# Turning probabilities and xn by VectorE blocks and DRAM instead of on PE, in an attention and FFN block

## What is computed

```python
q, k, v = ln(x) @ Wq, ln(x) @ Wk, ln(x) @ Wv
scores = where(above_diagonal, -max, q @ k.T)          # per batch, 1024 x 1024
x = x + ln(softmax(scores / 16) @ v @ Wo)
x = x + ln(ln(x) @ W[idx] + b[idx])
```

## Time and profile before

| | |
|---|---|
| three runs | 425.57, 426.01, 428.9 us (median 426.01) |
| span of the profiled execution (its own run time is not listed apart) | 424.3 us |
| PE, PEld | 414.0, 393.2 us busy |
| VectorE (DVE), ScalarE (ACT), GpSimd (POOL) | 339.8, 299.1, 118.3 us busy |
| DMA | 18.46 MB in 18951 packets, mean 44 GB/s |

### The profile page before, as it was taken

How to read it: one execution, slowest core, us unless ns; L and a number is a source line. 1 busy time by engine, 2 the same in 40 slices (tenths; PEclk the granted TensorE clock), 3 DMA queues, 4 the chain that set the end, 5 groups by cost and what they waited for, 6 DMA issues and landing times.

```text
span 424.3 us, 9812 instructions
## 1 busy us (share of the span) xinstructions
PE 414.0 (98%) x3045; PEld 393.2 (93%) x3045; DVE 339.8 (80%) x1010; ACT 299.1 (71%) x854; POOL 118.3 (28%) x237
## 2 busy tenths in 40 slices
PE   7999999999999999999999999999999999999993
PEld 7789999999999999999999999999999999999993
DVE  4578778987898878887788878898788887876776
...
DMA packets 18951, 18.46 MB, mean 44 GB/s; under 512 B 1140, under 2 KB 18932, under 8 KB 18932
## 3 DMA queue, kind: packets, MB, share of 16 engines
q1 hardware_dynamic: 18660, 17.96, 13.5%
...
...
## 4 chain that ended last, share of the span: by engine, by line
PE 93%; DMA 2%; ACT 2%; DVE 1%; issue 0%; POOL 0%; SPq 0%; POOLq 0%; DVEq 0%
PE bank L805 54%; PE score L805 23%; PE bank L908 7%; PE bank L932 3%; PE bank L819 3%; DMA wq<-in_L_attn_Wq_dram 1%; DMA bias_raw<-in_L_ffn_b_dram 1%; PE score L891 1%; PE score L847 0%; PE bank L865 0%; POOL f_rstd L387 0%; PE score L835 0%; DVE out_sb L778 0%; ACT squares_junk L591 0%; ACT sums_junk L470 0%
## 5 line engine op out<-in xcount | busy, mean ns | idle before, releaser
L387 POOL TENSOR_TENSOR o_rstd<-o_ve,minus_half 128x1 f32<-128x1 f32 x64 | 35.2, 550 | 193.8 <-DVE o_ve L735 193.8
L805 PE MATMUL bank<-v_hi,pT_lo 128*128 128x256 f32 x288 | 84.6, 294 | 0.0
L805 PE MATMUL bank<-v_hi,pT_hi 128*128 128x256 f32 x288 | 81.4, 283 | 0.0
L805 PE MATMUL bank<-v_lo,pT_hi 128*128 128x256 f32 x288 | 81.3, 282 | 0.0
L805 PE MATMUL score<-xT_hi,g_lo 128*128 128x384 f32 (+4 forms) x176 | 63.7, 362 | 0.0
L805 PE MATMUL score<-xT_hi,g_hi 128*128 128x384 f32 (+4 forms) x176 | 61.1, 347 | 0.0
L805 PE MATMUL score<-xT_lo,g_hi 128*128 128x384 f32 (+4 forms) x176 | 61.1, 347 | 0.0
L549 ACT ACTIVATE probs<-neg_scores,neg_max 128x128 f32<-128x128 f32 (+3 forms) x64 | 49.7, 776 | 14.0 <-DVE neg_max L707 13.5
L805 PEld LDWEIGHTS bank<-v_lo,pT_hi 128*128 128x128 f32 x288 | 55.0, 191 | 0.4
L805 PEld LDWEIGHTS bank<-v_hi,pT_lo 128*128 128x128 f32 x288 | 54.9, 191 | 0.3
L805 PEld LDWEIGHTS bank<-v_hi,pT_hi 128*128 128x128 f32 x288 | 54.9, 191 | 0.0
...
## 6 DMA issues: line engine op xcount, KB each, us to landing
x_sb<-in_L_attn_x_dram SPq DMA_DIRECT2D x32, 256.0 KB, 2.7
out_dram<-out_sb SPq DMA_DIRECT2D x31, 256.0 KB, 2.1
wq<-in_L_attn_Wq_dram ACTq DMA_DIRECT2D x1, 256.0 KB, 4.1
wk<-in_L_attn_Wk_dram SPq DMA_DIRECT2D x1, 256.0 KB, 4.4
wv<-in_L_attn_Wv_dram SPq DMA_DIRECT2D x1, 256.0 KB, 4.2
wo_raw<-in_L_attn_Wo_dram SPq DMA_DIRECT2D x1, 256.0 KB, 4.5
wf_raw<-in_L_ffn_W_dram SPq DMA_DIRECT2D x1, 256.0 KB, 2.7
...
```

What stands on the lines that cost most here:

```text
L387: return nc.gpsimd.tensor_tensor(dst[:, n0:n1], ve[:, n0:n1], minus_half[:, n0:n1], ALU.pow)
L805: last = nc.tensor.matmul(dst, l, r, start=(i == 0), stop=(i == len(passes) - 1))
```

## The change

The probabilities of a row tile (but for tiles 4 to 7 of the last batch) and the xn of batches 1 to 7 no longer pass PE. VectorE transposes them in blocks of 32 x 32 (steps **Q** n and **B** p). SP writes the blocks of a pair (of all xn) to DRAM, and reads them back in four issues of 32 partitions each, with the blocks in their places. In SP's table **P** p and **Q** p are write and read of a pair of probability rows, **W** and **R** those of xn, **A** p a load of x and **Z** p a store. ScalarE then rounds pT_hi out of SBUF (**P** n), and GpSimd subtracts pT_lo (**P** n in its table) in VectorE's place; xT_hi and xT_lo (**X**) come from SBUF too. **L** is parted into the statistics and the means (**K** p).

y is transposed as it is, without yn. The scale y_rstd is applied where the bias is added (F), now two operations of 256 columns, and the mean falls out because the FFN's weights have their column means subtracted once, by a matmul with a matrix of 1/256 and a subtraction in batch 0. The values get a 257th column root(256 eps) and a 258th of zeros, so that O's 257th column is the row sum times that root. One square with its sum then gives variance and eps together, and o_ez, the row sum of E, o_ve and f_ve fall away; f_sb has such a column too. x_ve, x_nm and y_ve move to GpSimd. out_sb is gone: Z writes f_sb, and F waits for the store of a batch before.

The tables are new. A mark ' puts a step into the batch after its own: O6, O7, Y1 to Y3 and F0 to F3 of a batch now stand among the scores of the next one. All 8 batches are written out.

```diff
-    PE_ORDER = """S0 V0 S1 V1 T0 S2 T1 S3 O0 V2 T2 O1 S4 T3 V3 O2 S5 O3 T4 S6 T5 S7 X0 Y0 O4 T6 O5 T7 O6 X1 Y1
-        O7 F0 G0 Y2 X2 F1 X3 F2 Y3 G1 G2 F3 G3"""
...
-    POOL_ORDER = """C0 L0 L1 C1 C2 C3 N0 N1 C4 L2 C5 L3 C6 N2 C7 N3 U0 U1 U2 U3"""
...
+    PE_ORDER = """S0 S1 S2 S3 O6' O7' S4 Y1' V0 S5 Y2' F0' O0 S6 S7 O1 F1' V1 V2 Y3' F2' O2 V3 F3' O3 O4 O5 G0 G1 G2 Y0 G3"""
...
+    DVE_ORDER = """G2' M0 M1 G3' Q0 Q1 M2 Y0' M3 L0 L1 K0 K1 Q2 Q3 L2 K2 B0 R6' R7' M4 B1 Y1' Q4 V0 B2 M5 L3 F0' K3 Q5 Y2'
+        M6 N3' B3 Z0' M7 R0 R1 F1' Q6 V1 V2 Q7 Y3' F2' Z1' N0 R2 V3 F3' Z2' R3 N1 X0 X1 X2 X3 R4 R5 Z3'
+        G0 N2 G1"""
+    POOL_ORDER = """P7' L0 L1 C6' L2 C7' P0 P1 C0 L3 U0' P2 P3 N3' C1 U1' C2 P4 P5 U2' C3 N0 U3' N1 C4 C5 N2 P6"""
+    SP_ORDER = """P0 Q0 P1 A3' Q1 P2 W0 Z0' Q2 A0 R0 P3 Z1' Q3 A1 Z2' A2 Z3'"""
...
+            def fetch(raw, kept, loaded):
+                for q, source in enumerate(kept):
+                    sp.dma_start(raw[q * QUAD:(q + 1) * QUAD].rearrange("a (i r) -> a i r", i=QUADS), source
...
+                    elif kind == "W":
+                        sp.wait_ge(x_turned, b.count(NP, 0))
+                        sp.dma_start(x_kept.rearrange("p q r -> p (q r)"), x_turn[:, :]).then_inc(x_written, 16)
+                    elif kind == "R":
+                        sp.wait_ge(x_written, b.count(16, 0))
+                        fetch(x_turn[:, :], x_kept.rearrange("(i a) q r -> q a i r", i=QUADS), x_raw_loaded)
+                    elif kind == "P":
+                        sp.wait_ge(p_turned, b.count(NT, 2 * n + 2))
+                        sp.dma_start(p_kept[n].rearrange("p q r -> p (q r)"), p_slot(n)).then_inc(p_written[n], 16)
+                    elif kind == "Q":
+                        sp.wait_ge(p_written[n], b.count(16, 16))
+                        fetch(p_slot(n), p_kept[n].rearrange("(i a) q r -> q a i r", i=QUADS), p_loaded[n])
...
-                        pool.wait_ge(o_ve_ready, b * NT + n + 1)
-                        rstd(o_rstd, o_ve, n, n + 1).then_inc(o_rstd_ready, 1)
+                        pool.wait_ge(o_squares, b.count(NT, n + 1))
+                        rstd(o_rstd, o_ss, n, n + 1).then_inc(o_rstd_ready, 1)
+                    elif kind == "P":
+                        pool.wait_ge(p_hi_ready, b.count(NT, n + 1))
+                        nc.gpsimd.tensor_tensor(p_half(pT_lo, n), p_quads(n), p_half(pT_hi, n).bitcast(f32),
+                                                ALU.subtract).then_inc(p_lo_ready, 1)
...
-                                             bias=neg_max[:, n:n + 1],
-                                             accum_out=exp_sums[:, n:n + 1]).then_inc(probs_ready, 1)
+                                             bias=neg_max[:, n:n + 1]).then_inc(probs_ready, 1)
+                    elif kind == "P":
+                        act.wait_ge(p_loaded[n // 2], b.count(QUADS * 16, QUADS * 16))
...
+                        nc.scalar.activation(p_half(pT_hi, n), p_quads(n), ACT.Identity).then_inc(p_hi_ready, 1)
...
+                            act.wait_ge(x_raw_loaded, b.count(QUADS * 16, 0))
+                        nc.scalar.activation(split_block(xT_hi, c, k), raw_block(c, k),
+                                             ACT.Identity).then_inc(x_hi_ready, 1)
...
-                        nc.scalar.activation(squares_junk[:, 0, n, :], cols(job.bank, D), ACT.Square,
-                                             accum_out=o_ss[:, n:n + 1])
-                        nc.scalar.activation(o_ez[:, n:n + 1], exp_sums[:, n:n + 1], ACT.Square,
-                                             scale=EPS ** 0.5).then_inc(o_squares, 1)
-                    elif kind == "K":
-                        act.wait_ge(y_shift_ready, b * NP + n + 1)
-                        for t in range(t0, t1):
-                            last = nc.scalar.activation(yn[:, p, t % 2, :], y[:, t, :], ACT.Identity,
-                                                        bias=y_shift[:, t:t + 1], scale=y_rstd[:, t:t + 1])
-                        last.then_inc(yn_ready, 1)
+                        nc.scalar.activation(squares_junk[:, 0, n, 0:D + 1], cols(job.bank, D + 1), ACT.Square,
+                                             scale=D ** -0.5, accum_out=o_ss[:, n:n + 1]).then_inc(o_squares, 1)
...
+                turned = x_turn[:, :].rearrange("p (q k t s) -> p t k q s", q=QUADS, k=KC, t=NT)
+                for t in (2 * p, 2 * p + 1):
+                    last = nc.vector.transpose(turned[:, t], xn[:, t, :].rearrange("p (k q a) -> p k q a", k=KC, q=QUADS))
+                last.then_inc(x_turned, 1)
...
+                    elif kind == "Q":
+                        dve.wait_ge(probs_ready, b.count(NT, n + 1))
+                        if b.known != 0 and not follows(in_dve, ("Q", n, b.known), ("R", n, b.known - 1)):
+                            dve.wait_ge(p_lo_ready, b.count(NT, n + 1 - NT))
+                        nc.vector.transpose(p_quads(n), probs[:, n % 2, 0:(n + 1) * PART].rearrange(
+                            "p (u q a) -> p u q a", q=QUADS, a=QUAD)).then_inc(p_turned, 1)
...
+                        dve.wait_ge(x_hi_ready, b.count(2 * KC, n + 1 - 2 * KC))
+                        c, k = n // KC, n % KC
+                        nc.vector.tensor_tensor(split_block(xT_lo, c, k), raw_block(c, k),
+                                                split_block(xT_hi, c, k).bitcast(f32), ALU.subtract
+                                                ).then_inc(x_lo_ready[c], 1)
...
-                    elif kind == "C":
-                        dve.wait_ge(o_squares, b * NT + n + 1)
-                        nc.vector.tensor_scalar(o_ve[:, n:n + 1], o_ss[:, n:n + 1], 1.0 / D, o_ez[:, n:n + 1],
-                                                ALU.mult, ALU.add).then_inc(o_ve_ready, 1)
                     elif kind == "R":
-                        job = at("O", n)
-                        dve.wait_ge(o_rstd_ready, b * NT + n + 1)
+                        job = Job(b, "O", n)
+                        if b.known != 0 and n % 2 == 0:
+                            dve.wait_ge(out_ready, b.count(NP, n // 2 + 1 - NP))
+                        dve.wait_ge(o_rstd_ready, b.count(NT, n + 1))
...
+                        job = Job(b, "F", n)
+                        if b.known != 0:
+                            dve.wait_ge(out_sent[p], b.count(16, 0))
                         dve.wait_ge(bank_full[job.bank], job.used + 1)
-                        nc.vector.tensor_tensor(f_sb[:, p, here, :],
-                                                cols(job.bank, (t1 - t0) * D).rearrange("p (t d) -> p t d", t=t1 - t0),
-                                                bias[:, None, :].broadcast_to([PART, t1 - t0, D]),
-                                                ALU.add).then_inc(bank_drained[job.bank], 1)
-                    elif kind == "U":
-                        dve.wait_ge(f_squares, b * NP + n + 1)
-                        nc.vector.tensor_scalar(f_ve[:, t0:t1], f_ss[:, t0:t1], 1.0 / D, EPS, ALU.mult,
-                                                ALU.add).then_inc(f_ve_ready, 1)
+                        dve.wait_ge(y_rstd_ready, b.count(NP, n + 1))
+                        for t in range(t0, t1):
+                            last = nc.vector.scalar_tensor_tensor(out=f_sb[:, p, t % 2, 0:D],
+                                                                  in0=bank[job.bank][:, (t - t0) * D:(t - t0 + 1) * D],
+                                                                  scalar=y_rstd[:, t:t + 1], in1=bias[:, :],
+                                                                  op0=ALU.mult, op1=ALU.add)
+                        last.then_inc(bank_drained[job.bank], 1)
...
+            def ffn_column_means():
+                pe.wait_ge(wf_centred, 1)
+                for k in range(KC):
+                    last = nc.tensor.matmul(score[:, 1, 1, 0:D], averaging[:, :], wf[:, k, :], start=(k == 0),
+                                            stop=(k == KC - 1))
+                last.then_inc(wf_means_ready, 1)
...
+                        if b.known != 0 or n >= 2:
+                            pe.wait_ge(max_ready, b.count(NT, n - 1))
...
+                        job = Job(b, "O", n)
+                        if b.last and n in LAST_T:
+                            take_bank(job, Job(b, "T", n, len(t_groups(n)) - 1), Job(b, "V", n // 2))
+                        else:
+                            take_bank(job, *([Job(b, "V", n // 2)] if n % 2 == 0 else []))
+                            pe.wait_ge(p_lo_ready, b.count(NT, n + 1))
+                        if n == 0 and b.known == 0:
+                            pe.wait_ge(v_ends_ready, 1)
+                        product(cols(job.bank, DE),
+                                [both(pT_hi, pT_lo, ALL, n % PS, slice(t * PART, (t + 1) * PART)) for t in range(n + 1)],
...
-                        pe.wait_ge(yn_ready, b * NP + n + 1)
```

(12 more changed lines are left out.)

627 lines of the change are left out of this document (382 added, 245 removed).

## The result

The changed kernel takes **431.8 us** (median of 10 runs, 428.7 to 434.6) beside 425.9 us for the kernel before. The ratio is 1.012 (95% interval 1.010 to 1.015). I had forecast 398, a gain; it is a loss of 1.2%. The profiled execution took 428.95 us, one of the faster of the ten.

The account below looks back on a forecast made before the run. PE was taken to bound the kernel: floor 384.7 us, plus 8.5 for seven batches at 45.5 and 3 for batch 0, gave 396.2 of span and 398 us of time. Forecast 390 to 406 (chance 0.58), range 387 to 416.

Parts of the forecast that it names:

- What leaves PE: Transposes leaving PE's queue: 29.1 us of probabilities and 12.0 of xn; PE's floor 384.7 us, 44.3 in a middle batch.
- the whole sum: Middle batch: VectorE's 39.9 plus 2.3 idle, 1 for the port and about 2.3 of semaphore waits, 45.5 us.
- VectorE, 39.9 us a batch: VectorE's work: 41.9 less 11.1, plus 1.1 for f_sb and 8.0 for block transposes; 4.4 under PE.
- the prediction's sign: Sign of being right: VectorE over 90% busy.
- The 2.3 us of semaphore waits: Term added to VectorE's work in the sum for a middle batch, about 2.3 us.
- GpSimd, 9 us a batch: GpSimd's takeover of the pT_lo subtraction: 9 us taken between 4.3 and 12.9, not a bound by sum.
- The wait of R7' for o_rstd: VectorE held at R7' by GpSimd's in-order queue: 2 to 2.5 us idle in every batch.
- The shared port, 1 us: VectorE and GpSimd overlapping by chance on wide operations that read SBUF: 1 us a batch taken.
- The dearer case: Whole GpSimd subtractions holding up VectorE, four a batch at 1.5 us each: sum some 30 us higher, near 428.
- DMA: DRAM trips: 28 us of transfers in a 45 us batch, pair 3's round trip about 10 us, covered; batch 0 waits 3.
- a late pair 3 blocks ScalarE's in-order queue and pT_lo blocks o_rstd: Rival of two small delays, 5 us a batch together: 422 to 430 us; chance 0.05.
- The DMA case: Rival: reads back at 100 GB/s, DMA bounds, PE waits naming a DMA, 441 us; decides from 110 GB/s down; chance 0.08.

Follow-up runs that it names:

- e10: Changed kernel with xn transposed by TensorE again, ScalarE's G2 ahead of P6 and VectorE's Z1' ahead of Y3': 405.4 us, 0.951 of the kernel before.
- e3: Changed kernel with the DRAM trip of xn moving one eighth of its columns, all steps, issues and waits kept: 400.9 us, 0.941 of the kernel before.
- e4: Changed kernel with GpSimd's subtraction for pT_lo cut to the first quarter of each row, waits kept: 429.8 us, 1.010 of the kernel before.
- e1: Changed kernel with one ScalarE step moved, g's rounding G2 ahead of P6 and P7: 418.9 us, 0.984 of the kernel before.
- e13: Changed kernel with both DRAM trips undone, TensorE transposing all probabilities and xn, in a new untuned step order: 553.8 us, 1.304 of the kernel before.

## Why the prediction was wrong

**What leaves PE: right.** e10's dense batch of 46.2 us gives 44.5 for the change's work, against 44.3. And e3's batches of 45.7 us stand beside the 45.5 of the whole sum: with the transfers in time, what was added up for the engines holds.

**VectorE, 39.9 us a batch: right.** Measured 40.6. The transposes of probabilities took 43.2 us for 33,536 elements, 1.29 ns each where 1.17 was taken, and those of xn 1.48 each: 9.0 us a batch where 8.0 was taken. VectorE was 77% busy where the prediction's sign was over 90%, and did not bound the change. The 2.3 us of semaphore waits in the sum stood there without a row behind them, and no run takes them apart.

**GpSimd, 9 us a batch: a little low, and harmless.** 82.2 us for 33,536 elements is 11.3 a full batch, within the bounds; by the Trainium skill (GPSIMD Engine Reference, Performance versus the Vector engine) the estimate was 10.1, and the trace is a tenth above it. The wait of R7' for o_rstd was there in every middle batch, at about 1.45 us in place of 2 to 2.5:

```profile
233.12 0.48 DVE L948 SCALAR_TENSOR_TENSOR y<-bank,o_rstd,x_sb 128x256 f32<-128x256 f32 x1 [1.45 <-POOL o_rstd L503]
```

e3 has the same wait of 1.45 us and takes 400.9 us, so the loss did not hang on it; and by e4, little hung on the subtractions.

**The shared port, 1 us: about right for the change.** The pair of Z0' takes 1.45 us there in the middle batches where most take 0.87, and all of these operations together 31.6 us against 27.8 in e4, whose subtractions are short: half a us a batch. The dearer case that I set aside, in which VectorE is held up for most of a wide subtraction, came once the order had changed: 2.21 us in place of 0.88, and 8 us from one step moved in e10. It costs only where something waits for it: e3 has pairs of 2.2 us too, and is the fastest run.

**DMA: the step that failed.** The prediction set 28 us of transfers against 45 us of batch, and pair 3's "about 10 us" was "covered, if the rate holds". The rate held in the main: the stretches above from 196 to 210 average some 280 GB/s, where I had 313, though from 199 to 208, while the reads were under way, it was 228 with the engines full. What failed is the use of a mean. A store, pair 2's reads, an x load, the reads of xn and pair 3's write are ready within some 6 us of one another, and their 3.3 MB need 12 us. Pair 3 came back at 219, 17 us after its transpose and not 10. The trip of xn, put at nothing outside batch 0, came late too: TensorE waited 11.5 us for x in seven batches. The second half of the error is that I asked when O6' needs pair 3 (48) and gave ScalarE's place for P6 (43) as a time, not as a block: P6 stands ahead of G2, G2' ahead of M0, and S2 could have run 1.3 us into the batch. The cover was for the consumer, not for what is queued behind it.

The rival "a late pair 3 blocks ScalarE's in-order queue and pT_lo blocks o_rstd" came nearest in size (422 to 430, against 431.8) and had half of the cause; it had 5%. The DMA case looked for 110 GB/s or less in the reads; 228 is below the 313 taken, but twice that. Nor did its sign come: the prediction wanted TensorE's waits to name a DMA, and they named neg_max and xT_lo on VectorE, with xT_lo even among the signs of being right. Only the chain behind them led to the transfers.

**The size**, by the runs: of the 31 us between the change and e3, 13 go with the one ScalarE step (e1) and the rest with the wait for x and what follows from it. I did not separate these further. What the probabilities' trips give by themselves also stays open, since e13 failed.
